# Zero rows ahead of each expert's region, and last blocks moved back

## The chip, the cores and the metric

The kernel runs on one core of a Trainium2 chip: TensorE (PE), VectorE (DVE), ScalarE (ACT), GpSimd (POOL), and SyncE (SP), which only issues DMAs. The metric is the device time of one execution in microseconds (us). The profile shows one execution. Its span runs from the first to the last instruction.

## The reference

Cross attention, then a mixture of 32 experts, both with a residual. Cut to what matters:

```python
x = x + xattn(layernorm(x), ctx, ctx, mask, ...)     # x: 4 x 1024 x 256, 16 heads, context 77
xf = layernorm(x).reshape(4096, 256)
scores = sigmoid(xf @ gate_weight.T)                 # 32 experts in 8 groups
# best 4 groups by max, then best 6 experts in them; weights scaled to sum 2.5
for gu, dn, c in experts:                            # 32 of them, I = 128
    o = silu(xf @ gu[:I].T) * (xf @ gu[I:].T) @ dn.T
    acc = acc + c[:, None] * o
shared_out = (silu(xf @ sg.T) * (xf @ su.T)) @ sd.T  # SI = 256
return x + acc + shared_out
```

## The kernel before, in words

The 4096 tokens are 32 tiles of 128. A tile t is (batch t % 4, piece t // 4).

**Tile loop** (`over_tiles`). Every engine walks the same 38 steps and takes stages of several tiles in each. The order is written out by hand, once for each engine. A tile gets attention, the second norm, its six experts and the place of each of its rows within each expert's region. POOL then scatters the tile's normalised rows (`rowb`) six times to the DRAM tensor `rows`, one indirect DMA for each choice (L509). Tiles below `PACED` = 29 have a POOL memset ahead of each scatter (L499); the last three have none. Each expert owns a region of 4096 + 128 rows in `rows`, region e beginning at row 128 + 4224 e. SP meanwhile loads expert weights, 512 KB a tile.

**Blocks.** After the loop each expert's rows are cut into blocks of 128, at most 224 in all (`NTB`). A block's start and its expert stand in `table`. A region's last block is read whole, so the rows behind the region's last one must be zero. The kernel before finds where each region ends (`counts`, L957 and L958 on PE, `tails` L1318 on DVE) and has 32 blocks of zeros from `padrow` written there: `store_tails` (L321 to L333), 4 + 6 of them by SP and 4 + 6 + 6 + 6 by ACT, one lot after each of ACT's four tanh of L649.

**The table.** DVE works out the blocks' numbers (`begin_blocks`, `follow_blocks`) and leaves them in `tab`. SP stores it to `tabd` in DRAM (L409) and loads two rows of it back across partitions as `pc` (L412). DVE's `name_blocks` (L1378, 8 instructions) and PE's `lay_table` (L969, 16) make the table, and DVE's `read_table` writes it (L1383 to L1386).

**Shared part.** For the last two of eight pieces (s = 6 and 7) the shared expert's work is done here, between the steps of the table: PE `s_up` (L893) and `s_down` (L906), ACT tanh (L649), DVE `s_hidden` (L1325 and L1329, called first for s = 6 half 0 ahead of `follow_blocks`, then for 6 half 1 and 7 half 0 ahead of `name_blocks`) and `s_base` (L1337). The last 512 KB of down weights (`wdn`, experts 28 to 31) lie where x1 of piece 6 was, so SP's load (L385) waits for `base`, which `s_base` counts.

**Rows phase.** SP waits for the table, the zero blocks and all scatters, and asks for 12 blocks (L433), then for two tables of 512 KB (L448, `bcA` and `bcB`). PE goes through 112 pairs of blocks: transposes (L991), gate and up (L1007), down (L1019). ACT and DVE evict and lay weights. SP stores the results in `yrows` (L439). POOL gathers each token's six results (L546) once the blocks that can hold them are stored, and DVE adds them (L1464). DVE's first step of the gather addresses (L1391) waits for the two tables of L448 and stands ahead of the second pair's `hidden` (L1438).

## Time and profile before

| | us |
|---|---|
| median of 3 runs | 813.57 (811.62 to 813.82) |
| span of the profiled execution | 809.6 |
| PE busy | 734.4 (91% of the span) |
| POOL busy | 536.7 (66%) |
| DVE busy | 518.8 (64%) |
| ACT busy | 389.1 (48%) |

The profile gives no time of its own execution beside the span. The median of the runs is 4.0 us above the span. Busy shares are averages over stages. The tile loop ends at about 375 us, the rows phase begins at about 412 us, and between them no compute engine is busy all the time. So the stretch between is read by itself, by the chain of waits and the order of time.

### The profile page before, as it was taken

To read this page: it belongs to the slowest core of one execution; us is meant where nothing else is said; L and a number is where in the kernel's file an instruction comes from. 1 tells how busy PE (TensorE), PEld (TensorE's weight loads), DVE (VectorE), ACT (ScalarE), POOL (GpSimd) and SP (SyncE) were. 2 spreads that over 40 slices of the span, in tenths; PEclk is the share of its full clock that TensorE was granted. 3 is DMA by queue.
4 is the path that set the end of the run, shared out by engine and by line. 5 is a ranking of instruction groups with operands and counts; after the bars stand their busy time and mean duration, and the time that the engine had idled before them with its cause. 6 is when DMAs were issued, how large, how long until landed. Compare 5 with 4: busy or idle time off the path is not lost.

```text
span 809.6 us, 18582 instructions
## 1 busy us (share of the span) xinstructions
PE 734.4 (91%) x5770; PEld 650.9 (80%) x5770; DVE 518.8 (64%) x1619; ACT 389.1 (48%) x832; POOL 536.7 (66%) x794
## 2 busy tenths in 40 slices
PE   6899999999999999986389999999989999899970
PEld 3788898889888888853169999899989999788860
DVE  5887777777777777755145334666666686646673
ACT  2454544444444444420026666665555665556540
POOL 0116878788788778867400007688978888778875
PEclk9899999999999999877699999999999999999995
DMA  9223334433333322214566558798978899778872
GB/s 290 78 54 105 125 125 131 131 124 115 114 127 130 126 72 85 79 66 145 183 195 183 173 165 244 220 266 241 288 232 264 246 275 270 224 228 252 255 222 84
DMA packets 113919, 140.27 MB, mean 173 GB/s; under 512 B 17103, under 2 KB 100691, under 8 KB 113824
## 3 DMA queue, kind: packets, MB, share of 16 engines
q1 hardware_dynamic: 90568, 84.75, 34.0%
q0 software_dynamic: 18432, 50.36, 20.4%
q10 hardware_dynamic: 4824, 3.99, 1.5%
q8 instruction: 48, 0.79, 0.4%
q14 instruction: 47, 0.39, 0.2%
HBM read 75.98 MB, written 63.06 MB: 172 GB/s over the span
## 4 chain that ended last, share of the span: by engine, by line
PE 31%; POOL 30%; issue 20%; DVE 11%; another core or an unknown queue 3%; DMA 2%; SPq 1%; ACT 1%; DVEq 0%; POOLq 0%; ACTq 0%
POOL rows L509 19%; PE sc_ps L1007 16%; PE bank L1019 8%; POOL work L499 7%; PE sc_ps L991 4%; POOL rstd L519 2%; DVE work L1464 2%; DVE work L1483 2%; DVE firsts L1041 1%; DMA store<-in_x 1%; POOL work L546 1%; DMA work<-tabd 1%; DVE work L1438 1%; DVE work L1157 1%
## 5 line engine op out<-in xcount | busy, mean ns | idle before, releaser
L1007 PE MATMUL sc_ps<-work 128*128 128x128 f32 x1792 | 221.0, 277 | 4.4 <-issue 1.8
L1007 PEld LDWEIGHTS sc_ps<-work 128*128 128x128 f32 x1792 | 210.3, 193 | 6.9 <-issue 4.5
L546 POOL DMA_INDIRECT work<-yrows,dest x192 | 188.5, 982 | 36.1 <-POOL work L499 20.5
L509 POOL DMA_INDIRECT rows<-work,dest x192 | 187.7, 977 | 35.0 <-issue 34.8
L499 POOL MEMSET work<- 128x304 f32 (+1 forms) x366 | 137.3, 375 | 104.7 <-DMA yrows<-work 88.9
L1438 DVE TENSOR_TENSOR work<-work,sc_ps 128x256 f32<-128x256 f32 x112 | 46.9, 419 | 128.9 <-issue 72.5
L1019 PE MATMUL bank<-wdn,work 128*128 x448 | 116.7, 383 | 9.9 <-issue 5.3
L1019 PEld LDWEIGHTS bank<-wdn,work 128*128 128x128 f32 x448 | 76.5, 191 | 18.2 <-issue 12.3
L688 ACT ACTIVATE work<-bank 128x512 f32<-128x512 f32 x112 | 66.8, 597 | 40.6 <-PE bank L1019 22.5
L1464 DVE SCALAR_TENSOR_TENSOR work<-work 128x256 f32<-128x256 f32 x160 | 76.8, 480 | 10.8 <-DMA work<-yrows,dest 7.5
L596 ACT ACTIVATE work<-work 128x1232 f32<-128x1232 f32 x32 | 39.4, 1231 | 91.9 <-DVE work L1157 75.3
L666 ACT ACTIVATE work<-sc_ps 128x256 f32<-128x256 f32 x112 | 42.7, 382 | 81.4 <-PE sc_ps L1007 43.0
L661 ACT ACTIVATE work<-sc_ps 128x512 f32<-128x512 f32 x112 | 66.7, 596 | 28.6 <-PE sc_ps L991 17.5
L812 PEld LDWEIGHTS bank<-work 128*128 128x128 f32 x640 | 75.9, 192 | 1.8 <-issue 0.5
L679 ACT ACTIVATE work<-wgu 128x512 f32 x112 | 70.7, 632 | 8.4 <-issue 7.4
L812 PE MATMUL bank<-work 128*128 128x51 f32 x640 | 74.7, 272 | 0.0
L991 PE MATMUL sc_ps<-cst,work 128*128 128x128 f32 x448 | 67.8, 274 | 2.1 <-DMA work<-rows 2.1
L991 PEld LDWEIGHTS sc_ps<-cst,work 128*128 128x128 f32 x448 | 56.2, 142 | 14.0 <-issue 2.2
L605 ACT ACTIVATE work<-bank 128x512 f32<-128x512 f32 (+1 forms) x96 | 47.3, 525 | 39.0 <-PE bank L800 36.4
L519 POOL TENSOR_TENSOR rstd<-var,cst 128x1 f32<-128x1 f32 x32 | 18.1, 565 | 71.3 <-DVE var L1193 70.9
L1483 DVE COPY work<-wgu 128x512 f32 x112 | 56.3, 503 | 13.2 <-issue 12.6
L1149 DVE TENSOR_REDUCE mx<-sc_ps 128x8 f32<-128x616 f32 x64 | 50.7, 792 | 4.1 <-PE sc_ps L778 4.1
(168 smaller groups left out, 1105.0 us busy)
## 6 DMA issues: line engine op xcount, KB each, us to landing
work<-rows SPq DMA_DIRECT2D x224, 128.0 KB
yrows<-work SPq DMA_DIRECT2D x224, 128.0 KB
wgu<-in_egu SPq DMA_DIRECT2D x16, 512.0 KB
store<-in_x SPq DMA_DIRECT2D x8, 512.0 KB, 10.6
wdn<-in_edn SPq DMA_DIRECT2D x8, 512.0 KB
out<-work SPq DMA_DIRECT2D x32, 128.0 KB
rows<-work,dest POOLq DMA_INDIRECT x192
work<-yrows,dest POOLq DMA_INDIRECT x192
```

The costliest lines, as they stand in the source:

```text
L499: pool.memset(dead, 0.0).then_inc(S_["gap"], 1)
L509: pool.indirect_dma_start(rows[:, :], bass.IndirectOffsetOnAxis(ap=dest[:, t, k:k + 1], axis=0), rowb[:, m, :], None).then_inc(scat[m], 16)
L546: pool.indirect_dma_start(yg[:, g % RG, :], None, yrows[0:n * P, :], bass.IndirectOffsetOnAxis(ap=dest[:, t, k:k + 1], axis=0)).then_inc(l ...
L661: a.activation(xeT[:, m % 2, :], ps8[m % 2], ACT.Copy).then_inc(S_["xeT"], 1)
L679: a.activation(wst[1][m % 2], wgu[:, bass.ds(named.pop(2 * i + 1) * 512, 512)], ACT.Copy).then_inc(S_["laid1"], 1)
L688: a.activation(ye[:, i % YP, :], ps8[6 + m % 2], ACT.Copy).then_inc(S_["ye"], 1)
L812: last = mm(pv_ps[:, n0:n0 + 3 * PV], pT[:, c, :], vbd[:, m, c, :, :].rearrange("p a b -> p (a b)"), start=c == 0, stop=c == NCH - 1, skip ...
L991: last = nc.tensor.transpose(ps8[m % 2][:, (2 * w + k) * P:(2 * w + k + 1) * P], xe[:, j % RX, k * P:(k + 1) * P], ident)
L1007: last = mm(ps8[2 + m % 2][:, (2 * w + g) * P:(2 * w + g + 1) * P], wst[w][m % 2][:, k * 2 * I + g * I:k * 2 * I + (g + 1) * I], xeT[:, m ...
L1019: last = mm(ps8[6 + m % 2][:, w * D:(w + 1) * D], hid[:, m % 2, w * P:(w + 1) * P], wdn[:, bass.ds(e * D, D)], start=True, stop=True)
L1464: v.scalar_tensor_tensor(outb[:, t % 3, :], yg[:, g % RG, :], slotw[:, t % 2, k:k + 1], so_far, ALU.mult, ALU.add).then_inc(S_["part"], 1)
L1483: v.tensor_copy(wst[0][m % 2], wgu[:, bass.ds(named.pop(2 * i) * 512, 512)]).then_inc(S_["laid0"], 1)
```

## The change

The zero rows move from behind a region to ahead of it. The 128 rows ahead of a region's first row lie at a place that is known when the kernel is built, so SP writes them in eight DMAs of four regions each, in the tile loop, steps 24 to 31 (`st_pads`). An expert's last block is moved back so that it ends with the region's last row. It then overlaps the block before it, or, where an expert has fewer than 128 rows, the zero rows ahead. The `counts` products, the cast to `tails` and `store_tails` are gone. `begin_blocks` has five more small DVE instructions, which work out how far back, and `tab` and `tabd` have a fifth row, because a block's code for the row it starts at (`row`) and its code for naming (`code`) are no longer the same. On SP the load of the last down weights, with its wait for `base`, now stands behind the first twelve row loads.

```diff
-        def store_tails(eng, engine, part):
-            need(eng, "tail_rows", 0)
...
-            for r in starts:
-                eng.dma_start(rows[bass.ds(r, P), :], padrow[:, :]).then_inc(tails_st[min(part, 2)], 16)
...
-            sp.dma_start(rows[0:P, :], padrow[:, :]).then_inc(tails_st[0], 16)
...
+            ahead = rows[0:E * REGION, :].rearrange("(e r) d -> r e d", r=REGION)
+
+            def st_pads(t, m, s):
+                if t >= NT - E // 4:
+                    e0 = 4 * (t - NT + E // 4)
+                    sp.dma_start(ahead[0:P, e0:e0 + 4, :],
+                                 padrow[:, :].unsqueeze(1).broadcast_to([P, 4, D])).then_inc(pads_st, 16)
+
             def step(tile):
                 at_tile(tile, 0, ld_experts)
+                at_tile(tile, 0, st_pads)
             over_tiles(step)
 
-            store_tails(sp, mybir.EngineType.SP, 0)
             need(sp, "tab", 0)
             sp.dma_start(tabd.rearrange("q e t -> e q t"),
-                         tab[0:E, NT:5 * NT].rearrange("e (q t) -> e q t", q=4)).then_inc(S_["tab_st"], 16)
+                         tab[0:E, NT:6 * NT].rearrange("e (q t) -> e q t", q=5)).then_inc(S_["tab_st"], 16)
...
-            store_tails(sp, mybir.EngineType.SP, 1)
-            for s in range(SE, SB - 1):
-                need(sp, "base", s - SE, 2)
-                ld_down(E - NX + 4 * (s - SE))
             sp.wait_ge(S_["table"], 2)
-            for q in range(3):
-                sp.wait_ge(tails_st[q], 16 * ((5, 6, 22)[q]))
+            sp.wait_ge(pads_st, 16 * E // 4)
...
             for j in range(RX):
                 ld_tile(j)
+            for s in range(SE, SB - 1):
+                need(sp, "base", s - SE, 2)
+                ld_down(E - NX + 4 * (s - SE))
             need(sp, "base", SB - 1 - SE, 2)
-            ld_bc(1, bcA)
-            ld_bc(3, bcB)
+            ld_bc(2, bcA)
+            ld_bc(4, bcB)
...
                     a.activation(shg[:, h, :], ps8[2 * h], ACT.Tanh, scale=0.5).then_inc(S_["shg"], 1)
-                    if s < SE + 2:
-                        store_tails(a, mybir.EngineType.Activation, 2 + 2 * (s - SE) + h)
...
-            need(pe, "selcum", NT)
-            need(pe, "place", NT - 1)
-            mm(rk_ps, onesb[:, :], regionb[:, :], start=True, stop=False)
-            mm(rk_ps, onesb[:, :], selcum[:, :], start=False, stop=True).then_inc(S_["counts"], 1)
...
-            need(v, "counts", 0)
-            v.tensor_copy(tails[0:1, :], rk_ps[0:1, :]).then_inc(S_["tail_rows"], 1)
...
+                v.scalar_tensor_tensor(lack, total, float(P), cum_ps[:, NT:NT + 1], ALU.mult,
+                                       ALU.subtract).then_inc(S_["sch"], 1)
...
+                v.wait_ge(S_["sch"], 8)
+                ts(back, begun[0:E, :], total, lack, ALU.is_equal, ALU.mult).then_inc(S_["sch"], 1)
+                v.wait_ge(S_["sch"], 9)
+                v.scalar_tensor_tensor(row, back[:, 1:NT + 1], -float(E), code, ALU.mult, ALU.add).then_inc(S_["sch"], 1)
+                tt(thr[0:E, :], thr[0:E, :], back[:, 0:NT], ALU.subtract).then_inc(S_["sch"], 1)
+                v.scalar_tensor_tensor(differ, back[:, 1:NT + 1], -float(P), back[:, 0:NT], ALU.add,
+                                       ALU.subtract).then_inc(S_["sch"], 1)
...
-                ts(a_new, apart[0:E, :], float(P), -float(P), ALU.mult, ALU.add).then_inc(S_["tab"], 1)
+                v.scalar_tensor_tensor(a_new, apart[0:E, :], float(P), differ, ALU.mult, ALU.add).then_inc(S_["tab"], 1)
```

The order of instructions shows three places. First SP between the table's round trip and the first row loads, in the kernel before (`tabd` and `pc` are the table on its way, `wdn` the last down weights, ISA rows set an address):

```order
22 L409 DMA tabd<-work 32x4x32
23 L412 DMA pc<-tabd 128x2x8
24 L329 TENSOR_LOAD tails
25 L333 ISA
26 L333 DMA rows<-padrow 128x256
...
37 L385 DMA wdn<-in_edn 128x4x256
38 L358 TENSOR_LOAD table
39 L433 ISA
40 L433 DMA work<-rows 128x256
```

The same place on SP in the changed kernel, up to the two tables that follow the row loads:

```order
12 L395 DMA rows<-padrow 128x4x256 x8
13 L404 DMA tabd<-work 32x5x32
14 L407 DMA pc<-tabd 128x2x8
15 L346 TENSOR_LOAD table
16 L423 ISA
17 L423 DMA work<-rows 128x256
...
40 L423 DMA work<-rows 128x256
41 L372 DMA wdn<-in_edn 128x4x256
42 L438 DMA work<-tabd 128x1024 x2
```

Nothing but waits now stands between the load of `pc` and the first row load, and the down weights come twelve loads later.

ACT after the tile loop, in the kernel before (L649 is the tanh of the shared part, the first two of four are seen):

```order
324 L649 ACTIVATE work<-sc_ps 128x512
325 L329 TENSOR_LOAD tails
326 L333 ISA
327 L333 DMA rows<-padrow 128x256
...
334 L649 ACTIVATE work<-sc_ps 128x512
335 L329 TENSOR_LOAD tails
```

And in the changed kernel, where L652 and what follows is the rows phase:

```order
323 L619 ACTIVATE gexp<-bank 128x32
324 L642 ACTIVATE work<-sc_ps 128x512 x4
325 L652 ACTIVATE work<-sc_ps 128x512
326 L346 TENSOR_LOAD table
327 L670 ISA
```

The four tanh now follow each other, with no DMA between.

DVE behind the tile loop in the kernel before, from the cast of the region ends to the first `s_hidden` (L1325):

```order
920 L1318 CAST tails<-bank 1x32
...
925 L1349 CAST work<-work 32x33
926 L1351 TENSOR_TENSOR work<-work 32x32
927 L1352 TENSOR_SCALAR work<-work,cst 32x32
928 L1354 TENSOR_SCALAR work<-work,cst 32x32
929 L1325 SCALAR_TENSOR_TENSOR work<-work,sc_ps 128x512
```

And in the changed kernel, where L1309 is that `s_hidden`:

```order
924 L1335 CAST work<-work 32x33
925 L1337 SCALAR_TENSOR_TENSOR work<-work,bank 32x1
926 L1339 TENSOR_TENSOR work<-work 32x32
927 L1340 TENSOR_SCALAR work<-work,cst 32x32
928 L1342 TENSOR_SCALAR work<-work,cst 32x32
929 L1345 TENSOR_SCALAR work<-work 32x33
930 L1347 SCALAR_TENSOR_TENSOR work<-work 32x32
931 L1348 TENSOR_TENSOR work<-work 32x32
932 L1349 SCALAR_TENSOR_TENSOR work<-work 32x32
933 L1309 SCALAR_TENSOR_TENSOR work<-work,sc_ps 128x512
```

One instruction is gone ahead of it and five small ones have come.

## Rows read from the trace of the kernel before

**Rows 1.** Chain that ended last, transition: start us, us, what.

```profile
394.66 5.74 another core or an unknown queue
...
401.54 4.82 PE bank L969 x16
406.37 3.67 PE bank L906 x16
...
410.77 0.40 SPq L385
...
412.19 0.36 SPq L433
...
419.32 6.38 DMA work<-tabd
```

**Rows 2.** Order of time, ACT: start us, us, engine, line, work, [idle before <-releaser].

```profile
382.83 8.36 ACTq L333 DMA_DIRECT2D rows<-padrow  x5
393.35 0.60 ACT L649 ACTIVATE work<-sc_ps 128x512 f32<-128x512 f32 x1 [13.34 <-issue]
...
402.83 0.60 ACT L649 ACTIVATE work<-sc_ps 128x512 f32<-128x512 f32 x1 [8.89 <-issue]
```

**Rows 3.** Order of time, SP's queue, the same columns.

```profile
382.76 0.01 SPq L409 DMA_DIRECT2D tabd<-work  x1
383.46 0.14 SPq L412 DMA_DIRECT2D pc<-tabd  x1
387.65 13.11 SPq L333 DMA_DIRECT2D rows<-padrow  x6
```

**Rows 4.** Order of time, DVE, PE and POOL, the same columns.

```profile
376.13 0.17 DVE L1347 TENSOR_SCALAR work<-work 32x33 int32<-32x33 int32 x1
...
376.65 0.35 DVE L1352 TENSOR_SCALAR work<-work,cst 32x32 f32<-32x32 f32 x1
...
378.39 10.11 PE L893 MATMUL sc_ps<-store,wsgu 128*128 128x512 f32 x16 [1.24 <-DVE store L1329]
...
396.31 0.96 POOL L509 DMA_INDIRECT rows<-work,dest  x1 [0.30 <-issue]
...
407.01 0.26 DVE L1386 TENSOR_SCALAR table<-work 1x224 int32<-1x224 int32 x1
```

**Rows 5.** POOL's groups from 373.4 to 398: count, busy, mean ns, idle before.

```profile
L509 POOL DMA_INDIRECT rows<-work,dest x19 | 18.2, 960 | 5.7 <-issue 5.7
```

**Rows 6.** DMA view of 398 to 399 us, busy tenths in 40 slices.

```profile
DMA  9948884400000000000000000000000000000000
```

**Rows 7.** Order of time, start of the rows phase, columns as in Rows 2.

```profile
413.51 0.69 DVE L1337 TENSOR_TENSOR store<-bank,work 128x512 f32<-128x512 f32 x1 [1.04 <-PE bank L906]
...
415.27 1.17 PE L991 MATMUL sc_ps<-cst,work 128*128 128x128 f32 x6 [1.80 <-DMA work<-rows]
...
425.72 1.22 DVE L1391 SCALAR_TENSOR_TENSOR work<-place,work 128x1024 f32<-128x1024 f32 x1 [2.77 <-DMA work<-tabd]
```

**Rows 8.** Line 385, SP's loads of down weights: ns min/median/max, first and last start.

```profile
L385 SPq DMA_DIRECT2D wdn<-in_edn x8: 367/368/396, 209.7 to 410.8; - x8
```

**Rows 9.** Windows: length, busy of each engine, PEclk, DMA share, GB/s.

```profile
209.50:276.00 66.50, 66.50 (x605) 59.84 (x603) 50.10 (x186) 32.93 (x78) 53.60 (x83) 1.00 0.40 126
...
560.00:780.00 220.00, 209.25 (x1587) 195.22 (x1585) 142.68 (x334) 130.33 (x265) 183.92 (x268) 1.00 0.84 250
```

**Rows 10.** Chain that ended last, rows phase, columns as in Rows 1.

```profile
441.34 1.79 PE sc_ps L1007 x16
...
444.43 1.79 PE sc_ps L1007 x16
...
591.31 4.19 another core or an unknown queue
...
778.22 1.41 another core or an unknown queue
```

**Rows 11.** Waits from 430 to 810: us in total, times, longest.

```profile
POOL work L499 <- DMA yrows<-work: 88.9, 3, 86.9
```

More of the change, by code:

```diff
@@ L106, in build @@
     yrows = nc.dram_tensor("yrows", (NTB * P, D), fp32, kind="Internal").ap()
-    tabd = nc.dram_tensor("tabd", (4, E, NT), fp32, kind="Internal").ap()
+    tabd = nc.dram_tensor("tabd", (5, E, NT), fp32, kind="Internal").ap()
     with ExitStack() as ctx:
@@ L244, in build @@
         fresh, at = carve(work, at, [P, NT])
-        tab, at = carve(work, at, [P, 5 * NT])
+        tab, at = carve(work, at, [P, 6 * NT])
+        moved, at = carve(work, at, [P, 2 * NT + 2])
         run, at = carve(work, at, [P, 2, 2 * NT])
@@ L282, in build @@
                      "gate_add score sfc group expert sel rank place dest selcum "
-                     "counts tail_rows cum_ps fresh pos_ps sch tab tab_st tab_ld bc_ld named sch_ps table yaddr dest2 "
+                     "cum_ps fresh pos_ps sch tab tab_st tab_ld bc_ld named sch_ps table yaddr dest2 "
                      "ld_s up_ps th hidt dn_ps sbase sg_ps shg shh sy_ps base wnorm "
@@ L289, in build @@
         scat = [sem(f"scat{i}") for i in range(4)]
-        tails_st = [sem(f"tails_st{i}") for i in range(3)]
+        pads_st = sem("pads_st")
         ld_xe = [sem(f"ld_xe{i}") for i in range(RX)]
@@ L321, in build @@
         block = ctx.enter_context(nc.Block())
-        TAILS = [0, 4, 10, 14, 20, 26, E]
-        def store_tails(eng, engine, part):
-            need(eng, "tail_rows", 0)
-            lo, hi = TAILS[part], TAILS[part + 1]
-            _, starts = nc.values_load_multi_w_load_instructions(
-                tails[0:1, lo:hi], engines=(engine,), min_val=0, max_val=ROWS - P,
-                skip_runtime_bounds_check_because="a region's start and its count of rows stay in this range")
-            for r in starts:
-                eng.dma_start(rows[bass.ds(r, P), :], padrow[:, :]).then_inc(tails_st[min(part, 2)], 16)
         LEAD, LAG = 1, 6
@@ L458, in _ @@
                     need(sp, "yaddr", 1)
-                    ld_bc(2, bcB)
+                    ld_bc(3, bcB)
                 if n < NPR:
@@ L1338, in s_base @@
                        sy_ps[half].rearrange("p (b d) -> p b d", b=2), x1_pair(t), ALU.add).then_inc(S_["base"], 1)
-            pos1, code, a_old, a_new = (tab[0:E, (1 + i) * NT:(2 + i) * NT] for i in range(4))
+            pos1, row, code, a_old, a_new = (tab[0:E, (1 + i) * NT:(2 + i) * NT] for i in range(5))
+            back, lack, differ = moved[0:E, 0:NT + 1], moved[0:E, NT + 1:NT + 2], moved[0:E, NT + 2:2 * NT + 2]
+            total = begun[0:E, NT:NT + 1]
             begun_int = begun_i[0:E, :].bitcast(i32)
@@ L1361, in follow_blocks @@
                 for i in range(5):
[L1362 removed]
+                    v.wait_ge(S_["sch"], i + 13)
                     after = run[0:E, i % 2, :]
```

9 lines of the change are left out of this document (3 added, 6 removed).

## The prediction

> **What bounds the kernel now.** I read the page first: PE is busy for 91% of the span, so only a stretch where PE stands still can give much. The windows show none in the tile loop, of which I give 66.50 us, all of them busy on PE [rows 9]. The chain of waits shows one between about 375 and 427 us. I followed it backwards. The tables for the gather addresses land at 425.70 (419.32 + 6.38). They were asked for behind twelve row loads, of which the first goes out at 412.19. That load stands behind SP's load of down weights at 410.77, which had waited for `base`. `base` waited for PE's s_down from 406.37, that for lay_table from 401.54, and that for DVE, which sat until 400.40 (394.66 + 5.74) on something the profile can't name [rows 1].
>
> In order of time the origin comes out. ACT's third tanh, for piece 7 half 0, runs at 393.35 after 13.34 us idle put down to "issue". In that gap ACT's queue is still issuing zero stores, five of them over 8.36 us. The fourth tanh is again 8.89 us late [rows 2]. DVE can't name blocks before it has done that half, since `s_hidden(7, 0)` stands ahead of `name_blocks`. PE had finished the product that the tanh reads far earlier: L893 runs 378.39 to 388.50 for both halves [rows 4]. So ACT, held by its DMA issues, ended the chain's wait.
>
> Beside it POOL scatters on: 19 scatters from 373.54, each 0.96 us with 0.30 between [rows 5], the last one ending at 397.27 [rows 4]. Its bytes move until 398.2 [rows 6]. POOL's work isn't touched by the change, and the row loads wait for it before and after. It is what is late next.
>
> **The change part by part.** I take each time from the same execution.
>
> *Zero stores gone from ACT and SP (32 after the loop).* ACT's tanh now waits for PE only. SP is free when `tab` is ready.
>
> *Five DVE instructions more, one less, ahead of the first s_hidden.* The trace has none of these, so by the nearest rows: 0.17 us (L1347) to 0.35 us (L1352) each [rows 4], 0.9 to 1.8 us for five. I take 0.2 each, as most are of L1347's size, 1.0 us, less 0.2 for the cast that goes: +0.8. The two PE products that go are under 0.5 us and were hidden in the same wait.
>
> *The table.* PE's L893 starts at 378.39 + 0.8 = 379.2 and ends at 389.3. Its first half, and with it the tanh and the first instruction of `s_hidden(7, 0)`, is done by about 387. The second needs PE's end. `pc` is there: the store of `tabd` and its landing took 0.70 us (382.76 to 383.46) [rows 3], `tab` is ready near 381, and even at the slow pace of SP's stores (six in 13.11, 2.2 us each) both DMAs are done by 387. Before, PE's lay_table began 1.14 after DVE's wait ended (400.40 to 401.54), so at 390.4 now, plus 4.82 [rows 1] = 395.2. From there to the written table it is 0.9 us (406.36 to 407.27) [rows 1, 4]: 396.1.
>
> *What SP then waits for.* The scatters. The last bytes move at 398.2. The landing isn't seen, since SP was waiting for something else. Bounds: at once (398.3), or as long again as the whole store of `tabd`, 0.7 us (398.9). I take 398.8. This is 2.7 us behind the table, so the table and the DVE instructions cost nothing; they would from 3.5 us more. From the last wait to the first row load it took 412.19 - (410.77 + 0.40) = 1.02 us [rows 1]. First load: **399.8, against 412.19, 12.4 earlier.**
>
> *SP's new order.* The load of down weights costs 0.37 us to issue [rows 8], with the sequencer's step 0.45, and is now ahead of the tables. In the kernel before it was ahead of the first row load, but outside the distance that I carry over: first load to landed tables, 425.70 - 412.19 = 13.51. Its 512 KB now travel within that distance. Below: nothing, since its bytes shared the queues with the rows before too. Above: its own transfer, 2.1 us at the 250 GB/s of the rows phase [rows 9]. Half of it had hardly begun at 412.19, so I take 0.5. Tables at 399.8 + 13.51 + 0.45 + 0.5 = **414.3 against 425.70: 11.4 earlier.** DVE's L1391 waited 2.77 for them [rows 7] and holds the second pair's `hidden`, so the rows phase shifts by this term, provided that the rest comes as early. It does. PE starts s_down at 395.2; before, it took 7.8 from there to the last `base` (406.37 to 414.20) [rows 1, 7], so 403.0. The first rows land at 399.8 + 3.08 = 402.9, by the same distance as before (412.19 to 415.27) [rows 1, 7]. PE begins at 403.2, 12.1 earlier. `wdn` is asked for at 406.4, 8 us before the tables are there; if it lands late, the wait for the tables covers it.
>
> *Zero rows in the tile loop.* Eight DMAs of 512 KB on SP, one a tile. The trace has the same shape and size: the down weights, one a tile for seven tiles, 0.37 us to issue [rows 8]. In that stretch seven tiles took 66.5 us, and PE was busy for all of it [rows 9]. So 0 us, hidden under PE. The direction differs (store instead of load), which a rival below takes up. Nobody waits for them but SP at the end, 30 us later.
>
> *Moved blocks.* The number of blocks, of loads and of stores stays: 224 each. Starts at other rows of 1 KB cost nothing that I can see. 0 us.
>
> *The rows phase.* One pair takes 444.43 - 441.34 = 3.09 us on PE [rows 10]. POOL's gathers wait for stored blocks, 86.9 us for the first [rows 11], so they move with PE, and the tail too. All of the 11.4 should reach the end.
>
> **Sum.** 809.6 - 11.4 = 798.2 of span. The execution's own time isn't given; the median of the runs lies 4.0 above the span, and I carry the difference: **802.2**.
>
> **The Trainium skill, weighed.** In the rows, ACT's issues cost 13.34 and 8.89 us of delay [rows 2]. The page "DMA: Bandwidth & Descriptors", section "Issuing engines are not separate DMA queues", says that DMAs from several engines share the same 16 engines, and that issuing them elsewhere saves only the sequencer's time, usually small beside the DMA. By that rule ACT's ten stores ahead of the third tanh would cost about 10 x 0.37 = 3.7 us, the tanh would not have been late by much, and the removal would bring some 4 us, a median of 809.6. The trace disagrees: while POOL scatters, a store took 1.7 to 2.2 us to issue, and the engine stood still.
>
> **The rivals.**
>
> 1. *DVE's 5.74 us recur* (394.66 to 400.40) [rows 1]. They lie in POOL's stretch and end when SP and ACT move again too, so they may come from the scatters and not from the zero stores. If they come after 389.3 at the same length, the table is at 396.1 + 5.7 = 401.8, SP's first load at 402.8, and the gain 9.4 - 1.0 = 8.4: 805.2. If DVE is held to the same 400.40, the table is where it was, 407.27, the first load at 408.3, and the gain 3.9 - 1.0 = 2.9: 810.7. For: the same name of the wait. Against: both queues were full of zero stores then. 7% for each form.
> 2. *The gain is eaten in the rows phase.* The chain there has seven waits for an unnamed queue, the first of 4.19, the last of 1.41 [rows 10]. They don't hang on the start, but an ACT queue with 50 instructions less meets them elsewhere. Worth 3 us either way inside the main case; to take 9 or more and end at no change, 811.1 to 816, 4%.
> 3. *Slower: zero stores to DRAM in tiles 24 to 31 hold the scatters.* `norm2` of a tile waits until the scatters of the tile four earlier have landed. If the stores press these back, each tile is late by a store's 2.1 us at 250 GB/s [rows 9]: 8 x 2.1 = 16.8, less 11.4: 819.0. It decides from 1.4 us a tile on. Against it: weight loads of the same size at the same rate with a DMA share of 0.40 [rows 9], and three tiles (28 us) of slack. 3%.
>    The same page's row on HBM row pitch speaks for this rival: it gives half the rate at a pitch of 4 MiB between partitions. Here regions are 4.125 MiB apart and partitions 1 KB, so I'd expect it not to bite; no run here shows it.
>
> **How the numbers follow.** Main case 79%, around 802.2, its own range 798.5 to 806: landing 0.5 either way, the queue's 0 to 2 us, and 3 for the rows phase. Rival 1: 14%, faster in both forms, the second by a hair. Rival 2: 4% same. Rival 3: 3% slower. A measurement of this kernel tells about 0.3% (2.4 us, so 811.1 to 816.0 is no change). From the edge of the second form of rival 1, 2% goes to same. Faster 0.90, same 0.06, slower 0.04 (1% for what I don't see). The range must take in most of rival 1, so 798 to 810.
>
> **What would show it.** In the profile after: four tanh without a wait for "issue", the third near 386. The table written near 396, before the last scatter has landed. First row load at about 400, PE's first transposes at 403, DVE's wait for the tables ended near 414.3. PE busy in the last tiles as before, and 3.09 us a pair. Wrong would be: DVE idle until 400 again; POOL's last scatter later than 397; tiles longer than 9.5 us from tile 24 on; PE's first `down` waiting for weights.

## The result and the profile after

Each time below is read against P, the end of POOL's last scatter, since everything after it waits for the scatters. "Second down" is the start of PE's `down` for the second pair of blocks, from which on the rows phase runs at its own pace.

| | before | changed |
|---|---|---|
| median, same chip, 20 runs each | 813.47 us | 808.75 us (800.25 to 819.73) |
| ratio | | 0.9933, 95% 0.9907 to 0.9959: 5.5 us |
| profiled run, and its span | 811.62 and 809.6 | 800.61 and 798.4 |
| first row load after P | 14.92 us | 4.99 us |
| PE's first transposes after P | 18.00 | 12.06 |
| second down after P | 30.15 | 24.73 |

The change is faster, by about half of the 11.4 us that I forecast. The time lies inside my range. The two spans differ by 11.2 us, which looks like my forecast and isn't, for the trace of the changed kernel is of its second fastest execution. 3.8 us of the 11.2 stand ahead of P (397.27 before, 393.49 after), where nothing in the change shortens the work, and 2.0 us behind the second down (382.2 and 380.2 us from there to the end). I take both for spread between executions. Between P and the second down the traces differ by 30.15 - 24.73 = 5.4 us, and this is what the medians show. Executions more than 1.5% above the fastest of their kernel are left out of the ratios, and of the traces below only that of "hidden before table" is of such a one.

The stretch of the transition in the changed kernel, in order of time: start us, us, engine, line, work, [idle before <-releaser]. L642 is ACT's tanh, L956 and L897 PE's lay_table and s_down, L1373 DVE's name_blocks, L1378 the first instruction of read_table, L1313 and L1321 s_hidden and s_base, L423 SP's row loads, L372 the down weights, L438 the two tables.

```profile
375.88 0.35 SPq L404 DMA_DIRECT2D tabd<-work  x1
377.43 0.37 SPq L407 DMA_DIRECT2D pc<-tabd  x1
380.13 0.60 ACT L642 ACTIVATE work<-sc_ps 128x512 f32<-128x512 f32 x1 [11.55 <-PE sc_ps L884]
383.56 0.60 ACT L642 ACTIVATE work<-sc_ps 128x512 f32<-128x512 f32 x1 [2.84 <-issue]
384.24 2.66 DVE L1373 TENSOR_SCALAR work<-work,pc 128x224 f32<-128x224 f32 x8
384.79 3.19 PE L956 MATMUL bank<-work,cst 128*1 128x224 f32 x16 [1.26 <-issue]
387.90 3.72 PE L897 MATMUL bank<-wsdn,store 128*128 128x256 f32 x16
392.53 0.96 POOL L502 DMA_INDIRECT rows<-work,dest  x1 [0.30 <-issue]
396.66 0.38 DVE L1378 TENSOR_SCALAR work<-bank 1x224 int32<-1x224 f32 x1 [9.76 <-remote]
398.15 0.69 DVE L1313 SCALAR_TENSOR_TENSOR store<-work,sc_ps 128x512 f32<-128x512 f32 x1
398.48 7.09 SPq L423 DMA_DIRECT2D work<-rows  x12
399.59 5.13 PE L897 MATMUL bank<-wsdn,store 128*128 128x256 f32 x16 [7.96 <-DVE store L1321]
405.55 1.06 PE L977 MATMUL sc_ps<-cst,work 128*128 128x128 f32 x8 [0.83 <-issue]
405.62 0.42 SPq L372 DMA_DIRECT2D wdn<-in_edn  x1
406.10 0.97 SPq L438 DMA_DIRECT2D work<-tabd  x2
414.20 1.22 DVE L1386 SCALAR_TENSOR_TENSOR work<-place,work 128x1024 f32<-128x1024 f32 x1
```

Down to 387.90 this is the forecast chain, and earlier than forecast. ACT's tanh no longer stand behind DMA issues (383.56, against 402.83 in [rows 2]). PE ends lay_table at 387.98, where I had 395.2 (3.8 us of that is the earlier P). Then DVE stands for 9.76 us ahead of reading that table, 8.7 of them behind the end of lay_table, though nothing that it needs is late by the trace. It moves at 396.66, which is P + 3.17. In the kernel before, DVE's wait ended at 400.40, P + 3.13 [rows 1]. The chain (start us, us, what) has it as its longest piece:

```profile
386.90 9.74 another core or an unknown queue
396.66 0.39 DVE work L1378
```

Two things hang on that wait. SP's first row load comes at 398.48, which is P + 4.99 in place of the forecast P + 2.5. And PE's s_down for piece 7 waits until 399.59 for s_base, which stands behind read_table on DVE, so that PE's transposes begin at 405.55, although the first rows had been asked for 7 us earlier. The wait for the tables of the gather addresses [rows 7] is gone: L1386 at 414.20 waits for nothing, and the tables take about 4.7 us from the issue:

```profile
DMA to landing us min/median/max: 4.6/4.7/5.3
```

The trace of the kernel before has the same end of a wait on three engines. Of ACT's seven stores between the third and the fourth tanh six go out only from 400.29 on, and SP's last two from 400.30, where DVE's wait ended at 400.40:

```profile
394.00 0.69 ACTq L333 DMA_DIRECT2D rows<-padrow  x1
400.29 2.44 ACTq L333 DMA_DIRECT2D rows<-padrow  x6
400.30 0.47 SPq L333 DMA_DIRECT2D rows<-padrow  x2
```

From P + 3.0 on a store takes 0.4 us. So the fourth tanh was late less by the work of issuing (2.44 us) than by the hold that ended there.

What doesn't hold DVE can be seen in the DMA view of 387 to 396.6 us (busy tenths in 40 slices, packets, then by queue):

```profile
DMA  0009400077000590002920009400078000000000
DMA packets 288, 0.79 MB, mean 82 GB/s; under 512 B 96, under 2 KB 96, under 8 KB 288
q0 software_dynamic: 288, 0.79, 23.0%
```

The DMA engines are idle for three quarters of it, and only POOL's scatters use them. No packet of an instruction queue lies in it either, so nothing in this view speaks for late code.

### The profile page after: what moved, and what is told of

Same layout as the page of the kernel before. It is cut to its first block, busy times and chain, and to the rows that moved or that the text cites. A ratio compares the mean times of both kernels' runs of the same rounds, so it can differ in the third digit from the quotient of the medians.

```text
span 798.4 us, 18476 instructions
## 1 busy us (share of the span) xinstructions
PE 728.2 (91%) x5768; PEld 648.2 (81%) x5768; DVE 521.0 (65%) x1623; ACT 389.0 (49%) x832; POOL 537.9 (67%) x794
## 4 chain that ended last, share of the span: by engine, by line
PE 40%; POOL 30%; issue 14%; DVE 7%; another core or an unknown queue 3%; DMA 2%; ACT 1%; DVEq 0%; ACTq 0%; POOLq 0%; SPq 0%
PE sc_ps L993 20%; POOL rows L502 19%; PE bank L1005 10%; POOL work L492 7%; PE sc_ps L977 5%; POOL work L539 2%; POOL rstd L512 2%; PE sc_ps L884 1%; DVE firsts L1027 1%; DMA store<-in_x 1%; DVE work L1143 1%; DVE mx L1135 1%; PE bank L897 1%; DVE work L1478 1%
## 5 line engine op out<-in xcount | busy, mean ns | idle before, releaser
L1433 DVE TENSOR_TENSOR work<-work,sc_ps 128x256 f32<-128x256 f32 x112 | 47.0, 419 | 123.7 <-issue 67.6
L1459 DVE SCALAR_TENSOR_TENSOR work<-work 128x256 f32<-128x256 f32 x160 | 76.9, 480 | 12.3 <-DMA work<-yrows,dest 9.0
L657 ACT ACTIVATE work<-sc_ps 128x256 f32<-128x256 f32 x112 | 42.8, 383 | 81.6 <-PE sc_ps L993 33.2
L652 ACT ACTIVATE work<-sc_ps 128x512 f32<-128x512 f32 x112 | 66.7, 596 | 32.0 <-PE sc_ps L977 26.7
L1478 DVE COPY work<-wgu 128x512 f32 x112 | 57.8, 516 | 14.4 <-issue 13.5
```

The costliest lines, as they stand in the source:

```text
L652: a.activation(xeT[:, m % 2, :], ps8[m % 2], ACT.Copy).then_inc(S_["xeT"], 1)
L1459: v.scalar_tensor_tensor(outb[:, t % 3, :], yg[:, g % RG, :], slotw[:, t % 2, k:k + 1], so_far, ALU.mult, ALU.add).then_inc(S_["part"], 1)
L1478: v.tensor_copy(wst[0][m % 2], wgu[:, bass.ds(named.pop(2 * i) * 512, 512)]).then_inc(S_["laid0"], 1)
```

## The experiments

The experiments ran on five chips, each kernel 6 to 12 times. The kernel before took 781.7, 834.1, 810.6, 810.6 and 833.0 us there (medians of 23 to 35 runs); I name the chips by these times, the two of 810.6 as first and second. Ratios are to the kernel before on the same chip. The last three columns come from one trace each. A "hold" is a wait behind which the trace names no releaser. What the expectations from the second chip on have as theory A: POOL's last 18 scatters, which have no memset between them, hold the others. The rivals have letters of their own.

| kernel | chip | ratio, 95% | first load - P | 3rd and 4th tanh - P | 2nd down - P |
|---|---|---|---|---|---|
| changed | 782 | 0.9981 (0.9953, 1.001) | 2.5 | -14.3, -10.9 | 18.8 |
| + 24 DVE memsets | 782 | 1.0023 (0.9994, 1.0052) | 2.5 | -14.5, -11.1 | 19.3 |
| stores at old place | 782 | 1.0006 (0.9974, 1.0037) | 2.5 | -14.6, -9.6 | 19.8 |
| tile loop's stores twice | 782 | 0.999 (0.9964, 1.0015) | 2.5 | -13.5, -10.0 | 19.0 |
| before | 834 | 0.9982 (0.9944, 1.002) | 16.8 | 3.3, 7.7 | 32.1 |
| changed | 834 | 0.994 (0.9907, 0.9972) | 5.2 | -11.5, -4.5 | 23.4 |
| changed, all paced | 834 | 0.9924 (0.9884, 0.9964) | 2.5 | -15.8, -12.4 | 20.0 |
| before, weights late | 834 | 0.9996 (0.995, 1.0041) | 13.4 | 1.2, 6.4 | 29.9 |
| before, all paced | 811, first | 0.9838 (0.9795, 0.9882) | 2.8 | -15.2, -8.9 | 18.0 |
| hidden before table | 811, first | 0.9903 (0.9868, 0.9937) | 5.0 | -12.0, -8.6 | 25.1 |
| stores at old place | 811, first | 0.9952 (0.9916, 0.9988) | 5.1 | -12.3, -3.9 | 23.2 |
| 12 of 18 paced | 811, first | 0.9858 (0.981, 0.9907) | 2.5 | -15.7, -12.3 | 19.0 |
| before, all paced | 811, second | 0.9893 (0.9846, 0.9939) | 2.3 | -16.3, -9.9 | 17.1 |
| changed, all paced | 811, second | 0.9936 (0.9893, 0.998) | 2.5 | -16.3, -12.9 | 18.8 |
| hidden, base before table | 811, second | 0.9949 (0.9909, 0.9989) | 6.2 | -12.0, -8.5 | 23.2 |
| changed | 811, second | 0.9966 (0.9927, 1.0006) | 7.2 | -10.4, -1.8 | 26.1 |
| stores, register addresses | 833 | 1.0027 (0.9989, 1.0066) | 14.1 | 2.6, 7.2 | 32.5 |
| stores, known addresses | 833 | 0.9997 (0.9953, 1.0041) | 11.5 | -8.6, 3.3 | 30.3 |

### On the 782 chip

The changed kernel again:

> The changed kernel once more. D is the time from the end of POOL's last scatter to the second pair's first down product on PE: 30.2 us before, 24.7 us in the changed kernel's first trace. Theory A (an unnamed stall of DVE at a fixed place in its instruction stream holds the table until 3.1 us after POOL's last scatter): the stall is at read_table again, ends 3.1 us after the last scatter, D is 24.7, and the time is 5 to 6 us under before. Theory B (the first trace's stall was an accident): no such stall, the table is written before the last scatter lands, D near 17 to 20, and 10 to 12 us under before.

With 24 small memsets at the start of DVE's program, which move every later instruction's number:

```diff
+            for i in range(24):
+                v.memset(idle[:, i:i + 1], 0.0)
```

> 24 small memsets more at DVE's start, where it waits for its first input anyway, so that everything on DVE stands 24 instructions later in its stream. Theory A: the stall meets DVE 24 instructions earlier in the program, near follow_blocks or the shared part, not at read_table, and lasts until 3.1 us after the last scatter, so name_blocks and lay_table come behind it: D near 30, and no faster than before. Theory B2 (the stall belongs to read_table's wait for PE, wherever it stands in the stream): still at read_table, D 24.7.

The changed kernel with 32 zero stores of 128 KB, issued by SP and ACT after the loop as before, ahead of the regions, in place of the eight in the loop:

```diff
-                at_tile(tile, 0, st_pads)
+            for r in range(TAILS[part], TAILS[part + 1]):
+                eng.dma_start(rows[r * REGION:r * REGION + P, :], padrow[:, :]).then_inc(tails_st[min(part, 2)], 16)
...
+                    if s < SE + 2:
+                        store_tails(a, 2 + 2 * (s - SE) + h)
```

> The changed kernel with its zero rows written where before had them: 32 stores of 128 KB after the tile loop, 10 by SP and 22 by ACT between its tanh. If ACT's DMA issues are what held before: third tanh some 10 us later than in the changed kernel, D 28 to 31, and time as before. If the moved load of down weights and not the stores brought the gain: D near 25 and the time 5 us under before.

And with the zero stores of the tile loop doubled, the second ones to a tensor that nobody reads:

```diff
+                    sp.dma_start(ahead2[0:P, e0:e0 + 4, :],
+                                 padrow[:, :].unsqueeze(1).broadcast_to([P, 4, D])).then_inc(pads_st, 16)
```

> The changed kernel with each of the eight zero stores of the tile loop issued a second time, to a DRAM tensor that nobody reads. If the stores hide under PE: time as the changed kernel (within 1 us), tiles 9.5 us. If they press on the scatters (the rival of the prediction): tiles 24 to 31 longer, by up to 2.1 us each, time up to 17 us over the changed kernel; half of that would be what the change itself pays.

On this chip nothing is held. The changed kernel there, in order of time:

```profile
389.64 0.38 DVE L1378 TENSOR_SCALAR work<-bank 1x224 int32<-1x224 f32 x1 [0.99 <-PE bank L956]
395.25 0.96 POOL L502 DMA_INDIRECT rows<-work,dest  x1 [0.30 <-issue]
398.74 3.03 SPq L423 DMA_DIRECT2D work<-rows  x6
400.97 1.40 PE L977 MATMUL sc_ps<-cst,work 128*128 128x128 f32 x4 [4.26 <-DMA work<-rows]
```

DVE reads the table 6.6 us ahead of P and waits only for PE. The first load is at P + 2.5 and the transposes wait for nothing but rows. This is the course that I had forecast for the other chip, step for step: first load P + 2.5, and the second down 11.3 us earlier than the first trace of before has it (30.15 - 18.84). But it is no gain here, and the stores at their old place cost nothing either (1.0006). The memsets told nothing of the hold, since there was none to move. The doubled stores cost nothing. In the windows of 276 to 342 us, into which five of the eight fall, PE is busy for 0.8 us less of 66 with them than without (the columns as in [rows 9]; first doubled, then single):

```profile
276.00:342.00 66.00, 63.74 (x572) 56.34 (x564) 50.71 (x190) 31.46 (x72) 55.93 (x87) 0.97 0.47 158
```

```profile
276.00:342.00 66.00, 64.54 (x583) 56.89 (x583) 50.07 (x193) 31.41 (x73) 55.11 (x84) 0.97 0.36 125
```

### On the 834 chip

The kernel before and the changed kernel, unchanged:

> The kernel before, for a trace beside the others of this call. The first four runs were on a chip on which before took 781.7 us, 32 less than on the chip of the first traces. New theory C: the first chip served DMA issues and whatever DVE waited for slowly while POOL scattered, and only there do the stores hold ACT's tanh. On a chip of about 782 us: tanh 3 about 14 us before POOL's last scatter ends (P), table written before P, first row load at P + 2.5, the second pair's down at P + 19, so nothing to gain. On a chip of about 813 us: as the first trace, first row load P + 14.9, down P + 30.2. Theory D (the changed kernel gains on each chip, and noise hid it): on a 782 chip as well the first row load comes at P + 10 or later.

> The changed kernel on the same chip. On a 782 chip by C: no unnamed wait on DVE after the tile loop, first row load at P + 2.5, down of the second pair at P + 19, time equal to before within 1 us. On an 813 chip: DVE held until P + 3.1, first row load P + 5.0, down P + 24.7, 5 us faster.

The changed kernel with POOL's memset ahead of the last 18 scatters too:

```diff
-PACED = NT - 3
+PACED = NT
```

> The changed kernel with a POOL memset ahead of the last 18 scatters too. The step of a scatter goes from 1.27 to 1.49 us, so P comes 18 x 0.22 = 4.0 us later. If unpaced scatters hold DVE on an 813 chip (theory A): DVE's unnamed wait is under 3 us or gone, and the table is written before P. On a 782 chip: only the 4 us.

The kernel before, with only the load of the last down weights put behind the first twelve row loads:

```diff
-            for s in range(SE, SB - 1):
-                need(sp, "base", s - SE, 2)
-                ld_down(E - NX + 4 * (s - SE))
             sp.wait_ge(S_["table"], 2)
...
             for j in range(RX):
                 ld_tile(j)
+            for s in range(SE, SB - 1):
+                need(sp, "base", s - SE, 2)
+                ld_down(E - NX + 4 * (s - SE))
```

> Before with only the load of the last down weights moved behind the first twelve row loads. On a 782 chip, where base should come before P, nothing: 0 +- 1 us. On an 813 chip the first row load then waits for the table alone: P + 11 instead of P + 14.9, but down only some 1 us earlier than before, since the shared part still holds PE.

The kernel before is held here as in its first trace, with six stores in 16 us:

```profile
389.40 15.96 ACTq L333 DMA_DIRECT2D rows<-padrow  x6
406.81 0.60 ACT L649 ACTIVATE work<-sc_ps 128x512 f32<-128x512 f32 x1 [19.73 <-remote]
```

ACT moves again at P + 3.3. The six stores take up most of its 19.73 us, until P + 1.8. The changed kernel gains 0.6% once more. With the scatters paced its trace has no hold, and the second down is at P + 20.0 in place of 23.4, though P itself comes some 18 x (1.48 - 1.26) = 4 us later; both together gave no difference from the changed kernel that I can tell. The moved load by itself brings nothing that can be measured (0.9996), though its trace has the first row load 3.4 us and the second down 2.2 us sooner.

### On the first 811 chip

The kernel before with the one line `PACED = NT`:

> The kernel before, with a memset of POOL ahead of the last 18 scatters too. P is the end of POOL's last scatter. Theory A (the 18 unpaced scatters slow the issue of the zero stores and hold what DVE waits for): the zero stores go out at about 0.9 us each, the four tanh come by P - 9, the first row load at P + 2.5 to P + 4, the first down at P + 15 to P + 20; POOL ends 3 to 4 us later, so on a chip where the changed kernel gains 5 us, this one is faster than before by 4 to 8 us. On a chip where nothing is held, no gain or 2 us slower. Rival B (the zero stores hold ACT by themselves, whatever POOL does): ACT waits 10 us or more for its issues again, the third tanh comes after P, the first row load at P + 13 or later, and the time is the same or up to 4 us slower than before.

The changed kernel with s_hidden ahead of read_table:

```diff
             name_blocks()
+            s_hidden(SE + 1, 1)
             read_table()
```

> The changed kernel, with DVE's s_hidden for piece 7 half 1 ahead of the reading of the table. Theory A with the hold on DVE at the reading of the table itself: s_hidden runs before the hold, PE's s_down for piece 7 runs ahead of P, the first transposes come at P + 8 in place of P + 11 to P + 12 (the first row load stays at P + 5), and the first down at P + 18 to P + 21: 0 to 3 us faster than the changed kernel. Rival C (DVE is held at about the same time whatever its instruction is): s_hidden for piece 7 half 1 waits until P + 3 itself, and the first transposes and the first down are where they are in the changed kernel, within 1 us. On a chip where nothing is held, no difference between the two, and nothing is told apart.

The kernel with stores at the old place, as on the 782 chip:

> The changed kernel, with 32 zero stores of 128 KB each ahead of the regions, issued by SP and ACT at the places of the kernel before in place of the eight in the tile loop. Moved blocks, no counts, and the order of the row loads stay. Theory A, on a chip where the scatters slow the issues: a store takes 1.7 us or more to issue, the third tanh comes at P - 4 or later, the first down at P + 25 or later, and the time is that of the kernel before within 0.4%. Rival D (what the other parts of the change brought, the order of the loads or the missing counts, is the gain): the first down at P + 21 to P + 25 and 0.5% or more faster than before. On a chip where nothing is held: stores of 0.9 us, the first down at P + 15, as once before.

The changed kernel with `PACED = NT - 1`:

> The changed kernel, with 12 of the last 18 scatters paced and the six of the last tile not. Theory A: the scatters' backlog is smaller, so the hold on DVE is gone or under 3 us, and P comes 2 to 3 us later than with 18 unpaced. The first row load at P + 2.5 to P + 4, the first down at P + 15 to P + 19; 0 to 3 us faster than the changed kernel where that is held. Rival E (the last six alone fill the queues): the hold of 5 us or more stays, ending at P + 3, and the time is that of the changed kernel or 2 us above it.

The first of these decides. The kernel before, all 32 zero stores in their old places, is 1.6% (13 us, from six runs) faster with 18 memsets of 0.35 us more. Nowhere did the change by itself bring more than 0.7%. Its order of time:

```profile
388.74 2.12 ACTq L333 DMA_DIRECT2D rows<-padrow  x4
390.96 0.60 ACT L649 ACTIVATE work<-sc_ps 128x512 f32<-128x512 f32 x1 [5.74 <-issue]
392.99 0.26 DVE L1386 TENSOR_SCALAR table<-work 1x224 int32<-1x224 int32 x1
393.64 2.85 ACTq L333 DMA_DIRECT2D rows<-padrow  x6
398.87 0.97 POOL L509 DMA_INDIRECT rows<-work,dest  x1 [0.16 <-issue]
402.67 3.47 SPq L433 DMA_DIRECT2D work<-rows  x7
404.86 1.40 PE L991 MATMUL sc_ps<-cst,work 128*128 128x128 f32 x5 [5.42 <-DMA work<-rows]
```

A store takes 0.48 us to issue (2.85 for six), against 1.7 and 2.2 in [rows 2, 3]; the table is written 6.6 us ahead of P. Unpaced scatters don't slow the stores from their start: in the first trace of before ACT's first four took 0.47 us each beside them, 20 us ahead of P.

```profile
377.47 1.89 ACTq L333 DMA_DIRECT2D rows<-padrow  x4
```

The DMA view of 387 to 393 us in the kernel before and, below it, in this one says the same in bytes:

```profile
DMA packets 754, 1.08 MB, mean 181 GB/s; under 512 B 134, under 2 KB 608, under 8 KB 754
```

```profile
DMA packets 1645, 1.87 MB, mean 311 GB/s; under 512 B 237, under 2 KB 1510, under 8 KB 1643
```

The engines moved 311 GB/s here with scatters among it, so it wasn't their rate that held the stores at 181. Pacing 12 of the 18 does as well (0.9858, no hold), as theory A has it and rival E not.

The stores at their old place were a half miss for theory A. A store took 0.9 us, DVE was held for 7.2 us, and the second down came at P + 23.2, as rival D had it. Its time (0.9952) is like the changed kernel's on other chips (0.9933 to 0.9966), which didn't run on this one. So here most of the gain, if not all, came with the stores back in their old place, by whatever else differs: the order of SP's loads, the missing counts or the stores' known addresses. The edit to s_hidden was badly made: PE's s_down for piece 7 waits for s_base of piece 6, which I had left behind the reading, so its time tells nothing, and its rows only where DVE is held.

### On the second 811 chip

The kernel before, all scatters paced, and the changed kernel likewise:

> The kernel before with the last 18 scatters paced, beside the next kernel on the same chip. Theory A (the unpaced scatters hold the zero stores and the compute engines; the change shortens only what they hold): 1.0 to 1.7% faster than before where before is held, the first down at P + 15 to P + 20, and no hold. Rival F (the 1.6% measured on one chip was that chip's): within 0.5% of before, or a hold of DVE or ACT of 5 us or more in the trace.

> The changed kernel with the last 18 scatters paced. Theory A: the same time as the kernel before paced in the same way, within 0.3%, since with pacing both have their table some 7 us ahead of P and their first down at P + 15 to P + 20: the change is then worth nothing. Rival G (moved blocks, eight stores in place of 32 or the order of SP's loads are worth something of their own): 0.4% or more faster than the kernel before paced.

The changed kernel with two steps of DVE ahead of read_table, and then unchanged:

```diff
             name_blocks()
+            s_hidden(SE + 1, 1)
+            s_base(SE)
             read_table()
+            s_base(SE + 1)
```

> The changed kernel, with DVE's s_hidden for piece 7 half 1 and s_base for piece 6 both ahead of the reading of the table, so that PE's s_down for piece 7 no longer waits for an instruction behind that reading. Theory A with the hold at the reading of the table: table at P + 4 and first row load at P + 5 as before, but s_down for piece 7 done ahead of P, first transposes at P + 8 to P + 9, first down at P + 18 to P + 21, 1 to 4 us faster than the changed kernel. Rival C (DVE is held from about P - 6 whatever stands next, because the hold follows the time and not the instruction): the held instruction is one of s_base for piece 6 or another before the reading, s_down for piece 7 starts behind P + 3, and the first down stays at P + 21 or later, the time the same within 0.2%.

> The changed kernel, for comparison with the three on the same chip. Where before is held, 0.4 to 1.0% faster than before, DVE held until P + 3, first row load at P + 5, first down at P + 20 to P + 22. Theory A: 0.5 to 1.1% slower than the two paced kernels. Rival F: the same as they within 0.3%. On a chip where nothing is held, all four within 0.3% of before, the paced ones 0 to 0.4% slower.

The paced kernel before is 1.1% faster than before on this chip as well. Paced, the changed kernel is no better than the kernel before paced (medians 804.6 and 801.92, intervals that overlap): rival G falls, and the change is worth nothing that can be measured once the scatters are paced. Nor is the changed kernel clearly faster paced than unpaced, here (0.9936 and 0.9966) or on the 834 chip (0.9924 and 0.994). The traces say why: the hold that goes is worth 3.4 to 7.3 us behind P, and P itself comes some 4 us later. On this chip the intervals of the paced kernel before and the unpaced changed one just overlap (0.9846 to 0.9939, 0.9927 to 1.0006).

The hold doesn't belong to the reading of the table. With `s_hidden` ahead, and with `s_hidden` and `s_base` ahead, DVE stood at these rows (the kernel of the first 811 chip, then that of the second):

```profile
393.23 0.69 DVE L1313 SCALAR_TENSOR_TENSOR store<-work,sc_ps 128x512 f32<-128x512 f32 x1
401.17 0.38 DVE L1378 TENSOR_SCALAR work<-bank 1x224 int32<-1x224 f32 x1 [7.25 <-remote]
```

```profile
390.60 0.69 DVE L1313 SCALAR_TENSOR_TENSOR store<-work,sc_ps 128x512 f32<-128x512 f32 x1
398.49 1.29 DVE L1321 TENSOR_TENSOR store<-bank,wdn 128x512 f32<-128x512 f32 x2 [7.21 <-remote]
399.70 0.37 DVE L1378 TENSOR_SCALAR work<-bank 1x224 int32<-1x224 f32 x1
```

In both DVE ran on to P - 4.0, was held at the next instruction and went on at P + 3.2. Both held instructions take a product of PE (lay_table's, s_down's), and so does each of the other compute instructions that I saw held. The two instructions that DVE still ran, at P - 5.4 to P - 4.0, came at a time when in the first trace of the changed kernel it stood already. So for them a late word of PE's newest results fits as well as a stop of the engine, though it wouldn't hold stores; no run tells the two apart. So rival C was right on the place. Its time (0.9949, against 0.9966 for the changed kernel beside it) tells no difference. In the unchanged one ACT and DVE are held together, one step earlier, and released within 0.1 us of each other, this time at P - 1.7:

```profile
397.37 0.60 ACT L642 ACTIVATE work<-sc_ps 128x512 f32<-128x512 f32 x1 [8.09 <-remote]
397.44 0.69 DVE L1313 SCALAR_TENSOR_TENSOR store<-work,sc_ps 128x512 f32<-128x512 f32 x1 [7.44 <-remote]
```

### On the 833 chip

The kernel with stores at the old place, its addresses from registers as in the kernel before, and then as it was:

```diff
-            for r in range(TAILS[part], TAILS[part + 1]):
-                eng.dma_start(rows[r * REGION:r * REGION + P, :], padrow[:, :]).then_inc(tails_st[min(part, 2)], 16)
+            _, starts = nc.values_load_multi_w_load_instructions(
+                tails[0:1, TAILS[part]:TAILS[part + 1]], engines=(engine,), min_val=0, max_val=ROWS - P,
...
+            for r in starts:
+                eng.dma_start(rows[bass.ds(r, P), :], padrow[:, :]).then_inc(tails_st[min(part, 2)], 16)
```

> The kernel of the two runs with stores at the old places (the changed kernel, 32 zero stores of 128 KB from SP and ACT after the loop), but each store's address comes from a register that is loaded from a small table, as in the kernel before, with the same values. Theory H (what held ACT in the kernel before is the issue of DMAs at register addresses while the scatters run unpaced): stores of 1.6 us or more, the third tanh at P - 4 or later, the first down of the second pair at P + 28 or later, 3 to 8 us slower than the same kernel with addresses known at build, and the time of before within 0.3%. Rival J (the form of the address costs nothing; what differs is the rest of the change): stores of about 0.9 us, second down at P + 23 or less, both kernels within 1 us of each other. On a chip where nothing is held, the stores take 0.9 us in either form by J, and by H still 1.6 us or more but with less than 2 us of it in the time.

> The same kernel with addresses known at build, on the same chip: stores of 0.86 us as in its two earlier runs, the third tanh at P - 12 to P - 15, the second down at P + 20 to P + 23. Theory H: 3 us or more faster than the kernel with registers. Rival J: the same within 1 us.

First with registers, then with known addresses:

```profile
393.70 13.81 ACTq L333 DMA_DIRECT2D rows<-padrow  x5
409.69 0.60 ACT L648 ACTIVATE work<-sc_ps 128x512 f32<-128x512 f32 x1 [18.29 <-issue]
```

```profile
388.65 5.10 ACTq L328 DMA_DIRECT2D rows<-padrow  x6
397.99 0.60 ACT L643 ACTIVATE work<-sc_ps 128x512 f32<-128x512 f32 x1 [8.77 <-remote]
409.91 0.60 ACT L643 ACTIVATE work<-sc_ps 128x512 f32<-128x512 f32 x1 [11.33 <-remote]
409.98 0.69 DVE L1316 SCALAR_TENSOR_TENSOR store<-work,sc_ps 128x512 f32<-128x512 f32 x1 [10.68 <-remote]
```

A store costs 2.8 us with a register and 0.85 without, as theory H says. The last three of the five slow ones go out 4.2 us apart, and two of SP's at the same instants (402.61 on both, 406.81 and 406.82). But the 3 us or more of theory H don't appear: without registers ACT and DVE are held by the other wait, to P + 3.3, and the second down gains 2.2 us only (32.5 to 30.3). Both kernels take the time of before, and the 0.3% between them lies within their intervals. The changed kernel didn't run on this chip; on the like one of 834 us its gain was 0.6%. That speaks for the stores among the four tanh, in either form of the address, as what the change took away. The same kernel with known addresses had 0.5% on the first 811 chip, which speaks against it. How the gain divides between the stores and the rest of the change is not shown.

## Why the prediction was half right

**What bounds the kernel** was read rightly as a place: the gain lies in the transition. The cause was half read. I had seen that the scatters slow the stores, and took the stores for the thing to remove. The one line that paces the scatters, in the kernel before and on two chips, shows that the unpaced scatters are the cause and the stores one of the things that they hold. Whether it is the gap in time or the memset as such that helps, no run separates.

**The tanh and the table's making.** Right, and pessimistic: lay_table ended at P - 5.5, forecast P - 2.1 (395.2 for a P of 397.27).

**The number** lies in the range only because I had widened it for rival 1. The main case's own range, 798.5 to 806, missed 808.75.

**The step that failed** is "396.1" for the written table, "2.7 us behind the table" for the scatters, with the remark that "the table and the DVE instructions cost nothing". The table was written at 397.53 = P + 4.0, behind the scatters. I had one trace of a DVE wait that ended at P + 3.1 and priced its return at 14%, against it that both queues were full of stores then. But six of those stores went out in 2.44 us once the wait had ended. Of eleven traces with 18 unpaced scatters, on chips of 811 us and more, nine have an unnamed wait of 5 us or more on DVE or ACT, which mostly ends between P + 3.1 and P + 3.4 (the others at P - 8.6 to P - 1.7); in the other two ACT's own slow stores hold it until P + 1.2 and P + 2.6, and in the nine they make up most of one, ACT's 19.73 us in the kernel before on the 834 chip. Of the five traces with paced scatters (all 18 in four, 12 in one) none has such a wait. In the first trace of the changed kernel it is the second form of rival 1 ("held to the same 400.40"). Its price was off too: 2.9 us forecast, 5.4 behind P. It assumed that name_blocks and lay_table would again come after the wait; they came before, which left the table at P + 4.0 instead of P + 10.0.

**"It does"**, my two words on the rest coming as early, failed with it: s_down was forecast at 395.2 and its second half ran at 399.59, so that PE's first transposes came at P + 12.06 in place of P + 5.9. I had not named who stands behind read_table on DVE.

**The tables, 414.3**: they landed near 412 (the last asked for at about 406.6, plus 4.7 to 5.3) and nobody waited. The down weights ahead of them cost nothing.

**DVE's five instructions**: 0.14 to 0.29 us each, about 1 us, as forecast, and off the path. **Zero stores in the loop**: no cost, even doubled (on the 782 chip, 0.999); rival 3 is refuted, and nothing shows the bite of the row pitch that I had weighed there. **The rows phase** passed the gain on: rival 2 isn't needed. **The median above the span**: 4.0 assumed, 2.2 measured (800.61 for a span of 798.4). The traced run of before had been the fastest of three.

**The Trainium skill.** I set the trace against its page "DMA: Bandwidth & Descriptors", section "Issuing engines are not separate DMA queues" (the sequencer's time to initiate a DMA is usually small beside it). The runs bear out the trace for unpaced scatters on slower chips (1.7 to 2.8 us a store, register addresses) and the page for paced ones: 0.48 us, where stores of this size took 3.4 us (median) from issue to landing in the kernel with stores at the old place on the 782 chip. The page's rule gave a gain of 4 us, my trace-based sum 11.4; 5.5 was measured. The 4 came nearer by luck, since the gain wasn't short for the reason that the rule gives: the third tanh came 9.4 us earlier against P, and the hold took part of it back.

**What stays open.** What DVE and ACT wait for in the hold. It isn't DMA bandwidth and there is no instruction packet in it. Each held instruction needs a result of PE which by PE's own (modelled) rows had been ready. In the first trace of before SP's stores, ACT's stores and DVE go on within about 0.1 us of each other, so it is likely one thing that holds them; that is argued, not shown. Why the 782 chip has no hold is open too; the kernel before wasn't traced there, so that its stores went through unheld is argued from the ratio of 1.0006 alone.

## What to carry to other kernels

When a wait without a name ends at a fixed distance from another engine's last instruction (here P + 3.1), that engine is the suspect: pace it before removing what it holds. A small gap between indirect DMAs (here a memset of 0.35 us each) can be worth as much as a rewrite or more: the kernel before with `PACED = NT` was 1.1 and 1.6% faster than before on two chips, and nothing that ran beside it was clearly faster. And before "all of it reaches the end", list who stands in the queue behind each instruction of the chain.

## What the runs showed of the hardware

The same kernel takes 782 to 834 us on different chips. Most of this isn't the hold: from the second down to the end the changed kernel took 366.5 us on the 782 chip, 380.2 on the chip of the first traces and 402.6 on the 834 chip. Waits from 430 us on (us in total, times, longest), in the first trace of before, then in the changed kernel on the 782 chip:

```profile
DVE work L1438 <- issue: 72.5, 44, 4.1
ACT work L666 <- remote: 25.1, 11, 3.6
```

```profile
DVE work L1433 <- ACT work L657: 94.0, 73, 2.2
DVE work L1478 <- issue: 12.2, 12, 1.7
```

L1438 and L1433 are the same instruction, `hidden`. In this trace on the 782 chip neither it nor ACT's L657 (L666 before) has any such wait; the traces of all chips of 811 us and more have them (54 to 83 and 18 to 41 us in total). I have no run that tells why. A program that is tuned on one chip alone can be tuned to a wait that the next one doesn't have.
